# First attention of a four-layer kernel: one projection for two heads, and the keys' other halves copied by DMA

## The reference, cut to what matters

```
Q = (X @ Wq).reshape(n, s, 16, 64)
K = (X @ Wk).reshape(n, s, 16, 64)
V = (X @ Wv).reshape(n, s, 16, 64)
attn = softmax(einsum('bshe,bthe->bsth', Q, K / 8), axis=2)
A = gelu(einsum('bsth,bthe->bshe', attn, V).reshape(n, s, 1024))
return X + A @ Wpost
```

## Time and profile before

| what | value |
|---|---|
| median of 3 runs | 4901.8 us (4894.93 to 4905.52) |
| profiled execution, its own time | 4896.5 us |
| its span | 4894.8 us |
| busy over the span | PE 85%, DVE 64%, ACT 49%, POOL 16% |
| first attention, its first projection to its last block | about 46 to 2,040 us of the span |

### The profile page before, as it was taken

One profiled execution on the slowest core, in us unless ns is written; L12 is line 12 of the kernel. 1 busy time (PEld: TensorE's weight loads), 2 busy tenths in 40 slices (PEclk: granted clock), 3 DMA queues, 4 the chain that ended last, 5 costly groups with the idle time before them and its releaser, 6 DMA issues. The chain is left out here.

```text
span 4894.8 us, 67703 instructions
## 1 busy us (share of the span) xinstructions
PE 4164.5 (85%) x21727; PEld 2199.2 (45%) x21763; DVE 3141.2 (64%) x6705; ACT 2386.8 (49%) x4327; POOL 797.9 (16%) x809
## 2 busy tenths in 40 slices
PE   6999999999999999789499996994999975996037
PEld 4555555555555555434244443332343434443026
DVE  5666566656665666544688884756778868126944
ACT  3555555555555555434166673532666741442013
POOL 0000000000000000023222211322222110330224
PEclk9999999999999999899699997995889977997558
DMA  1000000000000000000132210002221200000023
GB/s 43 5 5 5 5 5 5 6 5 5 5 6 5 5 5 6 9 11 6 39 63 52 49 29 13 7 7 48 53 47 30 54 13 1 11 6 5 0 80 89
DMA packets 70705, 103.60 MB, mean 21 GB/s; under 512 B 16112, under 2 KB 53872, under 8 KB 65616
## 3 DMA queue, kind: packets, MB, share of 16 engines
q1 hardware_dynamic: 68032, 96.22, 8.8%
q0 software_dynamic: 2496, 5.18, 0.3%
HBM read 75.21 MB, written 27.16 MB: 21 GB/s over the span
## 5 line engine op out<-in xcount | busy, mean ns | idle before, releaser
L2004 ACT ACTIVATE a_p<-PS 128x512 f32<-128x512 f32 (+3 forms) x1536 | 671.7, 492 | 344.1 <-PE PS L1895 335.1
L2341 ACT ACTIVATE a_p<-PS,a_nmax 128x1024 f32<-128x1024 f32 x520 | 580.7, 1117 | 478.7 <-DVE a_nmax L2398 465.6
L2398 DVE TENSOR_REDUCE a_nmax<-PS 128x1 f32<-128x1024 f32 x520 | 637.0, 1225 | 253.8 <-PE PS L2255 251.2
L2078 DVE TENSOR_REDUCE a_nmax<-PS 128x2 f32<-128x1024 f32 (+3 forms) x640 | 572.6, 904 | 166.2 <-PE PS L1905 161.7
L2281 PEld LDWEIGHTS PS<-ident,a_p 128*128 128x128 f32 x4096 | 451.5, 141 | 312.4 <-issue 241.3
L2281 PE MATMUL PS<-ident,a_p 128*128 128x128 f32 x4096 | 550.6, 277 | 12.5 <-issue 11.8
L2268 PE MATMUL PS<-a_blk,a_vst 128*64 128x512 f32 x2048 | 545.3, 616 | 0.0
L2438 DVE COPY a_blk<-PS 128x512 f32<-128x512 f32 x512 | 352.2, 688 | 188.5 <-PE PS L2281 186.4
L1895 PE MATMUL PS<-a_qs,a_ks 64*128 64x512 f32 (+3 forms) x1536 | 416.5, 458 | 46.2 <-ACT a_p L2004 43.6
L2228 POOL TENSOR_TENSOR a_diag<-ident,a_rec 128x1024 f32<-128x1024 f32 x64 | 121.5, 1898 | 1816.0 <-DVE a_rec L2405 1816.0
L1932 PE MATMUL PS<-a_p,a_vst 128*32 128x256 f32 (+2 forms) x4608 | 394.3, 416 | 16.4 <-ACT a_at L2012 15.3
(11 more groups left out here) (359 smaller groups left out, 5766.6 us busy)
## 6 DMA issues: line engine op xcount, KB each, us to landing
a_qs<-a_split SPq DMA_DIRECT2D x128, 128.0 KB
a_ks<-a_split SPq DMA_DIRECT2D x128, 128.0 KB
a_wqk<-in_L_qk SPq DMA_DIRECT2D x33, 256.0 KB, 2.7
a_split<-a_high SPq DMA_DIRECT2D x32, 256.0 KB, 4.3
a_split<-a_low SPq DMA_DIRECT2D x32, 256.0 KB, 4.9
f_w<-in_L_w SPq DMA_DIRECT2D x32, 128.0 KB, 2.1
a_qs<-a_nmaxt SPq DMA_DIRECT2D x256, 4.0 KB
f_sel_f<-in_gate_rows SPq DMA_DIRECT2D x3, 1024.0 KB, 4.8
```

The costliest lines, as they stand in the source:

```text
L2004: act.activation(probs[:, x % RING, j, 0:WIDTH[s]], filled(("T", it, s, j))[:, 0:WIDTH[s]], ACT.Exp, scale=scale).then_inc(s_tf, 1)
L2078: last = dve.tensor_reduce(nm[:, it % 2, place, 2 * p:2 * p + 2, i % 4], ps[:, :, 0:rest], AX, ALU.max, negate=True)
L2341: act.activation(probs[c][:, j, i, :], score_ps[n % 2], ACT.Exp, bias=nmax[:, NS * c + n:NS * c + n + 1], accum_out=sums[:, c, n:n + 1]).t ...
L2398: dve.tensor_reduce(nmax[:, NS * c + n:NS * c + n + 1], score_ps[n % 2], AX, ALU.max, negate=True).then_inc(s_mx, 1)
```

## The change

- Weights: `wqk` holds each head's columns once, so 128 columns are two heads. A pair has two P's in place of four: P0 gives the queries of both heads (head 0 in rows 0 to 63, head 1 in rows 64 to 127), P1 the keys.
- H: each P gets two H's of 64 rows, one for each head, each written to the head's own rows.
- L: still four, each now of 64 rows. The queries' low part is read from the head's own rows and written to the other half of `qs`; the keys' low part stays in its own rows of `kl`. The order of the four is now queries of head 0 and 1, keys of head 0 and 1.
- New: the other halves of `kh` and `kl` are filled by four DMAs from SBUF to SBUF for each pair (`double_keys`), 64 rows of 4 KB each, two for each head, issued by SP after that head's H and after its L.
- Waits: P no longer waits for L. S0 waits for the second L and for both copies of head 0, S1 for the fourth L, and S4 for the copies of head 1.
- Order of `second`: B0 P0 L0, B1 L1 P1 W0 L2, B2 L3 W1, B3 W2 S0, B4 S1 W3, and from B5 on as before (B5 S2 W4 S3). L0 to L3 are VectorE's alone. ScalarE takes its two H's where a P stands.
- The loads of `wqk` are half as large (128 KB).

```diff
-        wqk, wv, wo = sb("wqk", [P, 2, 2, P]), ...
+        wqk, wv, wo = sb("wqk", [P, 2, P]), ...
...
-            second += [("B", kt)] + ([("P", kt)] + weighed if kt < 4 else
-                                     [("S", 2 * kt - 8)] + weighed + [("S", 2 * kt - 7)])
+            if kt < 4:
+                second += [("B", kt)] + [[("P", 0), ("L", 0)], [("L", 1), ("P", 1)] + weighed + [("L", 2)],
+                                         [("L", 3)] + weighed, weighed + [("S", 0)]][kt]
+            else:
+                scores = [("S", n) for n in (2 * kt - 8, 2 * kt - 7) if n]
+                second += [("B", kt)] + scores[:1] + weighed + scores[1:]
...
             def _(sp):
+                def double_keys(J):
+
+                    for h in range(2):
+                        own, other = (slice(0, WIDE), slice(WIDE, P))[::1 - 2 * h]
+                        sp.wait_ge(s_hi, J * 4 + h + 3)
+                        sp.dma_start(kh[other, h, :].bitcast(F32), kh[own, h, :].bitcast(F32)).then_inc(s_dp[h], 16)
+                        sp.wait_ge(s_lo, J * 4 + h + 3)
+                        sp.dma_start(kl[other, h, :].bitcast(F32), kl[own, h, :].bitcast(F32)).then_inc(s_dp[h], 16)
+
+                double_keys(0)
                 with sp.Fori(0, BATCH) as b:
                     with sp.Fori(0, PAIRS) as p:
                         it = b * PAIRS + p
-                        sp.wait_ge(s_pj, it * 4 + 4)
+                        sp.wait_ge(s_pj, it * 2 + 2)
...
                         sp.wait_ge(s_vp, it * 2 + 3)
...
+                        double_keys(it + 1)
...
-                def project(J, k, offset):
-
-                    if k == 0:
+                def project(J, r, offset):
+                    if r == 0:
                         pe.wait_ge(s_wq, 16 * (J + 1))
-                    h, r = k // 2, k % 2
-                    if k < 2:
-                        pe.wait_ge(s_P, J * 2 * NS + 2)
-                    else:
-                        pe.wait_ge(s_lo, J * 4 + k - 1)
+                    pe.wait_ge(s_P, J * 2 * NS + 2)
...
                     if c == 0 and n < 2:
-                        pe.wait_ge(s_lo, J * 4 + n + 3)
+                        pe.wait_ge(s_lo, J * 4 + 2 * n + 2)
+                    if c == 0 and i == 0:
+                        pe.wait_ge(s_dp[j], J * 32 + 32)
...
-                def split_high(J, k):
-                    h, r = k // 2, k % 2
-                    act.wait_ge(s_pj, J * 4 + k + 1)
-                    dst = (qs, kh)[r][:, h, :]
-                    act.activation(dst, score_ps[r], ACT.Copy, scale=scale if r == 0 else 1.0).then_inc(s_hi, 1)
+                def split_high(J, r):
+                    act.wait_ge(s_pj, J * 2 + r + 1)
+                    for h in range(2):
+                        own = slice(h * WIDE, (h + 1) * WIDE)
+                        act.activation((qs, kh)[r][own, h, :], score_ps[r][own], ACT.Copy,
+                                       scale=scale if r == 0 else 1.0).then_inc(s_hi, 1)
...
                 def split_low(J, k):
-                    h, r = k // 2, k % 2
+
+                    r, h = k // 2, k % 2
+                    own, other = (slice(0, WIDE), slice(WIDE, P))[::1 - 2 * h]
                     dve.wait_ge(s_hi, J * 4 + k + 1)
                     if r == 0:
-                        rows = qs[WIDE:, h, :]
-                        dve.scalar_tensor_tensor(rows, score_ps[0][WIDE:], scale, rows.bitcast(F32), ALU.mult,
-                                                 ALU.subtract).then_inc(s_lo, 1)
+                        dve.scalar_tensor_tensor(qs[other, h, :], score_ps[0][own], scale, qs[own, h, :].bitcast(F32),
+                                                 ALU.mult, ALU.subtract).then_inc(s_lo, 1)
                     else:
-                        dve.tensor_tensor(kl[:, h, :], score_ps[1], kh[:, h, :].bitcast(F32),
+                        dve.tensor_tensor(kl[own, h, :], score_ps[1][own], kh[own, h, :].bitcast(F32),
                                           ALU.subtract).then_inc(s_lo, 1)
```

More of the change, by code:

```diff
@@ L2157, in attention0 @@
     s_pj, s_hi, s_lo = sem("a0_projected"), sem("a0_high_parts"), sem("a0_low_parts")
+    s_dp = [sem(f"a0_keys_doubled_{h}") for h in range(2)]
     s_vp, s_vd, s_va = sem("a0_values"), sem("a0_values_by_vector"), sem("a0_values_by_scalar")
@@ L2172, in sb @@
             return ctx.enter_context(nc.sbuf_tensor(f"a0_{n}", s, dt))
-        wqk, wv, wo = sb("wqk", [P, 2, 2, P]), sb("wv", [P, P]), sb("wo", [P, PAIRS, P])
+        wqk, wv, wo = sb("wqk", [P, 2, P]), sb("wv", [P, P]), sb("wo", [P, PAIRS, P])
         ones = sb("ones", [P, WIDE])
@@ L2211, in _ @@
                         it = b * PAIRS + p
-                        sp.wait_ge(s_pj, it * 4 + 4)
-                        sp.dma_start(wqk[:].rearrange("p h r f -> p (h r f)"),
-                                     d["L0_qk"][bass.ds(p + 1, 1)].rearrange("a p h r f -> p (a h r f)")).then_inc(s_wq, 16)
+                        sp.wait_ge(s_pj, it * 2 + 2)
+                        sp.dma_start(wqk[:].rearrange("p r f -> p (r f)"),
+                                     d["L0_qk"][bass.ds(p + 1, 1)].rearrange("a p r f -> p (a r f)")).then_inc(s_wq, 16)
                         sp.wait_ge(s_vp, it * 2 + 3)
                         sp.dma_start(wv[:], d["L0_v"][bass.ds(p + 1, 1)].rearrange("a p f -> p (a f)")).then_inc(s_wv, 16)
+                        double_keys(it + 1)
+                for h in range(2):
+                    sp.wait_ge(s_dp[h], 32 * (BATCH * PAIRS + 1))
                 sp.wait_ge(s_wv, 16 * (BATCH * PAIRS + 1))
@@ L2232, in _ @@
             def _(pe):
-                def project(J, k, offset):
-                    if k == 0:
+                def project(J, r, offset):
+                    if r == 0:
                         pe.wait_ge(s_wq, 16 * (J + 1))
-                    h, r = k // 2, k % 2
-                    if k < 2:
-                        pe.wait_ge(s_P, J * 2 * NS + 2)
-                    else:
-                        pe.wait_ge(s_lo, J * 4 + k - 1)
+                    pe.wait_ge(s_P, J * 2 * NS + 2)
                     for c in range(2):
-                        mm = pe.matmul(score_ps[r][:, c * CH:(c + 1) * CH], wqk[:, h, r, :],
+                        mm = pe.matmul(score_ps[r][:, c * CH:(c + 1) * CH], wqk[:, r, :],
                                        t.HT[:, bass.ds(offset + c * CH, CH)], start=True, stop=True)
@@ L2285, in _ @@
                 pe.wait_ge(s_one, 1)
-                for k in range(4):
-                    project(0, k, 0)
+                for r in range(2):
+                    project(0, r, 0)
                 for n in range(NS):
@@ L2309, in _ @@
                                     project(it + 1, n, after)
-                                elif c == 0:
+                                elif what == "S" and c == 0:
                                     score(it, 1, n)
-                                else:
+                                elif what == "S":
                                     score(it + 1, 0, n)
@@ L2346, in _ @@
                 act.sem_inc(s_ea, 1)
-                for k in range(4):
-                    split_high(0, k)
+                for r in range(2):
+                    split_high(0, r)
                 for n in range(NS):
@@ L2442, in _ @@
                                         invert_sums(it, c)
-                                elif what == "P":
+                                elif what == "L":
                                     split_low(it + 1, n)
@@ L2519, in heads @@
     def heads(name):
-        return a(name).reshape(P, 8, 2, 64).transpose(1, 0, 2, 3)
+        return a(name).reshape(P, 8, P).transpose(1, 0, 2)
     wrap = np.arange(9) % 8
-    qk = np.stack([heads("L0_attn_Wq"), heads("L0_attn_Wk")], 3)
-    out["L0_qk"] = c(np.concatenate([qk, qk], 4)[wrap])
+    out["L0_qk"] = c(np.stack([heads("L0_attn_Wq"), heads("L0_attn_Wk")], 2)[wrap])
     out["L0_v"] = c(a("L0_attn_Wv").reshape(P, 8, P).transpose(1, 0, 2)[wrap])
```

## The result

The changed kernel took 4821.3 us in the median (4807.3 to 4837.4, 4 runs), the kernel before 4903.1 us beside it. The ratio is 0.9837 with a 95% interval of 0.9804 to 0.987, against the forecast's 0.985 and 4827 us. The profiled execution has a span of 4821.7 us, 73.1 us less than the 4894.8 us of the kernel before.

What follows compares the result with a forecast made beforehand. PE was taken to bound the first attention: 3.78 us a pass removed, less 0.85 and 0.54 lost, gives 76.5 us over 32 passes; with 1.5 us lost at the start, 4827 us, ratio 0.985, range 4800 to 4865.

Steps and rivals of the forecast that it cites:

- The bound: First attention, pass c = 1: PE sets the pace, so a step taken from it shortens the pass.
- Two P's removed: Pass c = 1 on PE: two P's at 1.89 us each go, 3.78 us a pass, at most 121 us.
- VectorE's order: Pass c = 1: L1 and L2 stand ahead of VectorE's copy of B2, so B3 loses 0.85 us.
- The copy: DMA into `kl` of head 0 before S0: lands 3.1 us after issue, so 0.54 us is lost.
- The sum: Whole kernel: 4896.5 - 76.5 + 1.5 = 4821.5 us in the profiled execution, 4827 us as median forecast.
- Rows: H's and L's: half the rows save no time, VectorE 1.23 us either way, 1.03 us taken for ScalarE.
- The start: Chain ahead of the loop: S0 1.2 us later, a loss of 1.5 us taken, between 0 and 3.
- ScalarE's copy of B4: Pass c = 1, after the exponentials: done at 1017.7, needed by B5's transposes at 1017.87, close but in time.
- The other side: S0's copy makes the kernel slower: at 6.2 us the pass loses 0.7 us, 4926 us; chance 0.06.
- the slow copy: Copy into `kl` takes 4.0 to 5.3 us, pass gains 1.49 to 0.19 us: 4855 to 4897 us; chance 0.12.
- The clock rival: Waits at B3 and S0 let PE's clock fall each pass, costing about 51 us: 4878 us; chance 0.06.

Runs made afterwards that it cites:

- e9: Changed kernel with the matmuls of both P's issued twice, the second time onto the same result: 4930.7 us, ratio 1.006 to the kernel before.
- e1: The changed kernel again with no edit, as control: 4828.6 us, ratio 0.985 to the kernel before.
- e2: Changed kernel with S0 moved behind B4: 4812.0 us, ratio 0.9817 to the kernel before.
- e5: Changed kernel without the loop's four key copies for each pair, first pair's copies kept: 4811.2 us, ratio 0.980 to the kernel before.
- e6: Changed kernel with each loop copy moving only columns 0 to 511, 128 KB in place of 256 KB: 4810.9 us, ratio 0.9808 to the kernel before.
- e3: Changed kernel with L2 moved behind VectorE's copy of B2, L3 following it: 4884.1 us, ratio 0.9959 to the kernel before.
- e4: Changed kernel with keys projected before queries and the queries' two L's behind B2's copy: 4804.4 us, ratio 0.9792 to the kernel before.
- e8: Changed kernel with L2 and L3 behind B2's copy and also S0 behind B4: 4828.0 us, ratio 0.9846 to the kernel before.

## Why the prediction was right

**The bound.** Right. PE's steps set the pace: the work that the change took away costs 2.81 us a pass when e9 puts it back.

**Two P's removed, priced at 3.78 us a pass.** The term was too large: 3.44 us. I took a P as B and P together less B, with B alone at 0.85 us read in front of a score. Where a P goes, B is followed by W, and that step takes 975.25 - 974.23 = 1.02 us in the changed kernel. So a P costs 2.74 - 1.02 = 1.72 us, which e9 shows directly at 1.71. The ceiling inside the loop was 110 us, not 121.

**VectorE's order, B3 0.85 us late.** Right in place and cause. W1 to B3 takes 1.63 us in place of 1.01, so it is 0.62 late and not 0.85.

**The copy, 3.1 us, S0 0.54 us late.** It lands after 3.24 us, and W2 to S0 takes 1.60 us in place of 1.01, 0.59 late. By the figures of the Trainium skill, "SBUF — State Buffer", Door 1: The DMA port swizzle (the rate) and The DMA setup-cost knee (the 2 us), I had an estimated 3.3 us, and the trace is between the two.

**The sum.** 3.44 - 0.62 - 0.59 = 2.23 us by these steps and 2.25 for a whole turn, where 2.39 was forecast. The P's were 0.34 too high and B3's wait 0.23 too high, and that these two nearly cancel is not luck: both hold the same misread step, a B before a W taken as 0.85 us where it is 1.02. The forecast of the time did not hang on it. It set S0 by the chain L2, DMA, S0 at 1013.45 - 1001.99 = 11.46 us after B0, and 11.62 was measured, 0.14 of the difference being the copy's.

**Where it was luck.** The gain of the loop was forecast at 76.5 us and is 72.0. The stage still ended 77.3 us earlier, because the turns at a batch's end happened to be fast in that profile; e1's ended 68.2 us earlier with the same passes. The stages behind differ by up to 29 us between executions. That the median came within 6 us of 4827 is therefore closer than the mechanism accounts for.

**What the sum hid.** It lists two waits as two losses, as if either could be saved alone. S0's could: e2, e5 and e6 took it away and B3's 0.62 us were what was left. B3's could not: S0's place is set by L2 and the DMA, and e3 took B3's wait away by a later L2 and lost 0.70 us. (No run frees B3's buffer earlier with L2 in its old place; that this gains nothing is read from the chain.) Only e4, which moves the L's of the keys forward and with them both waits, got back 1.2 us.

**Rows.** An operation on 64 rows takes as long as one on 128 on both engines: ScalarE's H's 1,018 ns after 1,025, VectorE's L's 1.22 after 1.23. The L that shifts rows takes 1.22 us, as does the one that does not.

**The start.** Forecast 1.5 us later. S0's first matmul moved from 56.76 to 58.11 us, where 58.0 was forecast, and then ran at the lower clock (1.19 us where it took 0.72). The first B0 of a pass c = 1 came 1.45 us later, and 1.09 in e1.

**ScalarE's copy of B4.** No wait for it appeared; B5 followed W3 at 1.01 us.

**The rivals.** The other side and the slow copy did not occur: the longest wait for the copy was 0.5 us. The clock rival did not occur either, but the forecast's argument against it was too easy. The row just before that of the earlier trace rows, in the same scores of the kernel before, has the clock at 0.66, with gaps of 1.22 and 1.17 us in front of its scores:

```profile
60.00:65.00 5.00, 3.83 (x10) 2.49 (x8) 2.69 (x3) 2.50 (x5) 0.00 (x0) 0.66 0.00 0
```

The forecast compared the sum of the gaps with a window in which the gaps were many and short. e3 shows that one gap of 1.84 us was enough in 22 of 32 passes, 1.3 us more than the changed kernel's longest.

## What to carry to other kernels

Price a removed step by the distance between its neighbours once it is gone, not by one that another neighbour closes. When several waits lie in one pass, follow the chain that the last one hangs on before saving an earlier one: send off first what has a DMA behind it, and leave for later what a matmul reads without a DMA between. Where a wait for a DMA can't be avoided, put a step of TensorE's own work in the middle of it. Compare versions by distances inside a pass where whole times differ by chance as much as the change is worth.

## What the runs showed of the hardware

In e3, one unbroken wait of 1.84 us in front of S0 was followed by matmuls at the lower clock in 22 of 32 passes, 1.6 us each, some 35 us of that execution. In e8 S0 came as late, but PE's idle time was 0.62 us and 0.36 us with B4 between them, and the clock was 1.00. The stages behind the first attention, with the same code, took between 2861.9 (e1) and 2891.1 us (e5) in these profiles, and in one stretch with the same number of records the granted clock was 0.81 in e1 and 0.76 in e4. Turns at a batch's end took 75.6 us in one profile of the changed kernel and 78.7 in another. So differences below some 15 us of this kernel have to be read from the distances inside a pass. Four SBUF-to-SBUF copies of 64 rows by 4 KB for each pair slowed no engine; the copies of `kh` held that of `kl` up by 0.23 us, and all four held the load behind them up by 1.0 us.
